# An attention and mixture-of-experts layer on one core: the hand-written order at the seam of two attention stages is changed, with a DMA's queue and a normalisation's place

## The chip, the cores and the metric

The kernel runs on 1 core of one Trainium2 chip. The metric is the device time of one execution, in microseconds (us): median 461.74 of 3 runs (461.70 to 462.92).

## The reference, cut to what matters

```python
# x (8,112,256), ctx (8,375,256), 16 heads; all float32
x = layernorm(x + self_attention(x, w_qkv, w_out, b_out))        # head width 64
x = layernorm(x + cross_attention(x, ctx, ctx, mask, Wq, bq, Wk, bk, Wv, bv, Wo, bo))  # head width 16
logits = x @ router.T; e = argmax(logits)                        # 8 experts, top 1
x = layernorm(x + down[e] @ (silu(gate[e] @ x) * (up[e] @ x)) + shared_expert(x))
```

## The kernel before, in words

Each engine has its own program; semaphores join them, and an engine runs its program strictly in order. The order in which the pieces stand in each program is therefore the schedule. T = 896 tokens are 8 batch elements of 112 rows, or NT = 7 tiles of 128 rows.

**Self-attention** is a loop over b = 0..7 on every engine. In one pass TensorE (PE) does `score1(0,b)`, then `out1(b-2)` (the output projection of tile b-2, 16 instructions, from b = 2 on), `between1(b,0)`, `score1(1,b)`, `between1(b,1)`, then four `turn`s (transposes of the probabilities of four heads each) with `between1(b,2..5)` between them, `value1(0,b)` ahead of `turn(2)` and `value1(1,b)` at the end. `between1` holds work for later stages: for b < 6 the next q, k, v of self-attention; at b = 6 the first k and v of cross-attention; at b = 7 `turn_x1` of the first tiles (the transposed, normalised result), the first query projection `project_q(0)` and one `project_k`. VectorE (DVE) does `rowmax`, `normalise` (a reciprocal and a multiplication), `evac_pt` (copies a turned tile out of PSUM) and the layernorm of tile b-2 in two halves: `ln1_a` (add, statistics, eps; then GpSimd takes the inverse root) and `ln1_b`. ScalarE (ACT) does the exponentials `exps(g,b)` and copies out of PSUM: `evac_o`, `evac_x1`, `evac_k`.

`query_scale` on DVE (L1122) makes the factor by which `evac_q` multiplies the queries. It reads the result of one small matmul (L564), which lies in the same PSUM bank as `out1`'s; `prep` 7 says it is done, and `out1(0)` waits for it.

**Cross-attention** is a loop over 32 slots n = 4b + g. In a slot PE does `score2(n)`, `turn2_(n-1,0)` and `(n-1,1)`, work of place 0, `turn2_(n-1,2)` and `(n-1,3)`, work of places 1 and 2, `value2(n-2)`. Place 1 waits for `max2` of the slot's third strip (L671), since `project_v` of place 1 writes that strip's bank. DVE does four `mask_and_max(n,r)` with `between(n,place)` among them and then `evac_pt2(n-1)`, for which the next `score2` waits. ACT does the exponentials `exps2(n,r)` and three of the four `evac_pt`. For b = 0 `between_first` holds the rest of the queries' preparation: tiles 3 to 6 of `turn_x1` and `project_q(1)`. They share one PSUM bank (`PE_M2`), so each waits for the copy of the one before.

For b >= 1, in slot g = 2, DVE copies the former element's output (`evac_ot`), PE turns it (`turn_o`), and DVE divides it by its sums (`normalise2`, L1215: a reciprocal and a multiplication).

After that come the router, the shared expert, and a loop over the routed tiles; the change does not touch them.

The inputs come by DMA. SyncE (SP) issues nearly all: first eight parts of `wqkv`. ACT issues one, the first two batch elements of `xT`. The first matmul needs that and the first part of `wqkv`.

Of the kernel before, what the change touches and what calls it, by code (L numbers as in the profile page):

```python
# [20 lines left out]
B, S, C = 8, 112, 256  # L21
# [30 lines left out]
def build(nc, a, out):  # L52
    ctx = ExitStack()
    with ctx:
# [193 lines left out]
        def _(sp):  # L248
            for u in range(8):
                sp.dma_start(wqkv[:, :, 256 * u:256 * u + 256], a["wqkv"][:, :, 256 * u:256 * u + 256]).then_inc(w_qk[u], 16)  # L250
# [136 lines left out]
        def _(pe):  # L387
# [78 lines left out]
            def out1(t):  # L466
                pe.wait_ge(ot1[1], t + 2)
                pe.wait_ge(ot1[0], t + 2)
                if t == 0:
                    pe.wait_ge(w_loaded["out"], 16)  # L470
                    pe.wait_ge(prep, 7)
                else:
                    pe.wait_ge(y1, t)
                for k in range(8):
# [10 lines left out]
            def project_q(i, M=PE_M2):  # L485
                pe.wait_ge(x1t_sb, 5 if i == 1 else min(-(-(i + 1) * S_PAIR // TILE), NT))
# [20 lines left out]
            def between1(b, c):  # L507
# [18 lines left out]
                elif c == 2:  # L526
                    pe.wait_ge(x1t_sb, 1)
                    project_v(2, 0, J)
                elif c == 3:
                    project_q(0, J)  # L530
                elif c == 4:
                    pe.wait_ge(v_sb, KT)
                    project_k(0, 1, J)
                else:
                    pe.wait_ge(q_sb, 1)
                    turn_x1(2, J)
# [5 lines left out]
            for b in range(B):  # L542
# [19 lines left out]
                if b == 1:  # L562
                    pe.wait_ge(prep, 5)
                    pe.matmul(PE_W1[:, 0:S], anyw, ident[0:S, 0:S], start=True, stop=True).then_inc(q_any, 1)  # L564
# [3 lines left out]
            def score2(n):  # L568
# [3 lines left out]
                if n == 0:  # L572
                    pe.wait_ge(exp1[2], B)
                    pe.wait_ge(exp1[3], B)
                    pe.wait_ge(k_sb, KC + 1)
                    pe.wait_ge(x1t_sb, 3)
# [12 lines left out]
            def turn2_(n, r):  # L589
                pe.wait_ge(exp2, n * STRIPS + r + 1)  # L590
                if n == 0 and r == 0:
                    pe.wait_ge(pt1, 4 * B)
                elif n == 0 and r == 1:
                    pe.wait_ge(y1, NT)
# [52 lines left out]
            def between_first(g, place):  # L647

                if (g, place) == (0, 0):
                    pe.wait_ge(ot1[1], B)  # L650
                    project_k(1, 1)
                if (g, place) == (1, 0):
                    pe.wait_ge(k_sb, 2 * KC)
                    turn_x1(3)
                if (g, place) == (1, 2):
                    pe.wait_ge(x1t_sb, 4)
                    turn_x1(4)
                if (g, place) == (2, 0):
                    project_q(1)
                if (g, place) == (2, 2):  # L660
                    pe.wait_ge(q_sb, 2)
                    turn_x1(5)
                if (g, place) == (3, 0):
# [231 lines left out]
        def _(act):  # L895
# [41 lines left out]
            act.dma_start(xT[:, :, 0:S_PAIR], a["xT"][:, :, 0:S_PAIR]).then_inc(xT_loaded[0], 16)  # L937
            for c in range(2):
                evac_v(c, 0)
            for b in range(B):  # L940
# [16 lines left out]
                if b == B - 1:  # L957
                    evac_k(0, 1, PE_J1[0])
                    evac_x1(2, PE_J1[1])
# [15 lines left out]
            def before_exps(n):  # L975

                b, g = n // GROUPS, n % GROUPS
                if b == 0 and g >= 2:
                    evac_x1(g + 2)
# [3 lines left out]
            def between(n, place):  # L983

                b, g = n // GROUPS, n % GROUPS
                if (g, place) == (0, 0) and b == 0:
                    evac_k(1, 1)
                if (g, place) == (1, 0) and b == 0:
                    evac_x1(3)
                if (g, place) == (3, 0) and b == 0:  # L990
                    evac_x1(6)
# [478 lines left out]
```

## Time and profile before

| | |
|---|---|
| time, 3 runs | 461.74, 462.92, 461.70 us |
| the profiled execution: its own time / its span | 461.74 / 460.0 us |
| PE busy | 416.0 us, 90% of the span |
| DVE, ACT, GpSimd busy | 242.0, 194.8, 37.8 us |
| self-attention, about | 5 to 170 us |
| cross-attention, about | 170 to 340 us |

The page divides the span in 40 slices. A digit is the busy share of the slice in tenths:

```profile
PE   5998999999999988999999999999899999999910
DVE  1366666656656637575666565757724622222225
ACT  1063353433534528676666656676741010111200
PEclk9999999999999999999999999999999999999975
```

PE is the engine to watch. Its work overlaps itself (a matmul begins before the one ahead has ended), so a stretch is without gaps when the rows of PE follow each other with no bracket. A bracket at the end of a row is the idle time ahead of it and what ended that.

### The profile page before, as it was taken

The numbers are of one execution on the slowest core, as the hardware profiler recorded it, in microseconds if no ns is written. First come the engines' busy times: TensorE is split into PE (matmuls) and PEld (weight loads), VectorE is DVE, ScalarE is ACT, GpSimd is POOL, SyncE is SP. The second block draws the span as 40 slices with busy tenths as digits, with TensorE's granted clock in tenths as the row PEclk, the third lists the DMA queues.
The fourth block names the chain that finished last, engine by engine and source line by source line (L and its number), as shares of the span: only waits on it lengthen the run. The fifth ranks groups of instructions, "written<-read, shape, count | busy, mean of one in ns | idle before, by whom it ended". The sixth has DMA issues, their size and how long they took to land.

```text
span 460.0 us, 8866 instructions
## 1 busy us (share of the span) xinstructions
PE 416.0 (90%) x3119; PEld 294.9 (64%) x3120; DVE 242.0 (53%) x709; ACT 194.8 (42%) x580; POOL 37.8 (8%) x59
## 2 busy tenths in 40 slices
PE   5998999999999988999999999999899999999910
PEld 5865878778786766676666666766654656555510
DVE  1366666656656637575666565757724622222225
ACT  1063353433534528676666656676741010111200
POOL 3010010110101001000010100101000320000043
PEclk9999999999999999999999999999999999999975
DMA  7993000000000102124040406500000120111123
GB/s 257 359 389 107 1 1 1 0 2 1 1 1 1 34 21 119 66 105 167 8 170 3 171 2 216 232 1 1 2 1 0 36 70 11 36 35 46 34 68 114
DMA packets 16137, 33.29 MB, mean 72 GB/s; under 512 B 2096, under 2 KB 10784, under 8 KB 14816
## 3 DMA queue, kind: packets, MB, share of 16 engines
q1 hardware_dynamic: 15152, 30.68, 18.4%
q0 software_dynamic: 672, 1.84, 1.3%
q8 instruction: 25, 0.41, 0.4%
q10 hardware_dynamic: 272, 0.23, 0.2%
q14 instruction: 16, 0.13, 0.1%
HBM read 26.97 MB, written 5.77 MB: 71 GB/s over the span
## 4 chain that ended last, share of the span: by engine, by line
PE 78%; DVE 9%; issue 4%; DMA 3%; POOL 3%; ACT 2%; DVEq 0%; POOLq 0%; SPq 0%; ACTq 0%
PE bank L603 11%; PE bank L405 9%; PE bank L419 6%; PE bank L585 6%; PE bank L475 6%; PE bank L503 5%; PE bank L497 4%; PE bank L825 4%; PE bank L849 3%; PE bank L831 3%; PE bank L462 3%; PE bank L619 3%; PE bank L759 3%; PE bank L436 3%; PE bank L448 2%
## 5 line engine op out<-in xcount | busy, mean ns | idle before, releaser
L1199 DVE CUSTOM_DVE_ANT_0 p<-bank,mask 112x375 f32<-112x375 f32 x128 | 62.8, 546 | 33.7 <-PE bank L585 33.7
L965 ACT ACTIVATE p<-p,nm 112x375 f32<-112x375 f32 x128 | 74.7, 608 | 6.7 <-DVE nm L1199 6.7
L603 PEld LDWEIGHTS bank<-ident,p 112*125 112x125 f32 x384 | 48.9, 187 | 22.5 <-issue 18.0
L972 ACT ACTIVATE pT<-bank 125x336 f32<-125x336 f32 x96 | 42.8, 447 | 47.5 <-PE bank L603 47.5
L603 PE MATMUL bank<-ident,p 112*125 112x112 f32 x384 | 59.6, 287 | 1.3
L405 PE MATMUL bank<-x2T,arena 128*128 128x224 f32 x256 | 54.7, 362 | 5.2 <-DMA arena<-in_wqkv 5.2
L908 ACT ACTIVATE p<-bank,nm 112x112 f32<-112x112 f32 x128 | 43.6, 366 | 18.6 <-DVE nm L1073 18.6
L405 PEld LDWEIGHTS bank<-x2T,arena 128*128 128x128 f32 x256 | 47.9, 196 | 5.2 <-DMA x2T<-in_xT 4.8
L1066 DVE TENSOR_SCALAR arena<-bank 128x448 f32<-128x448 f32 x32 | 20.0, 624 | 28.7 <-PE bank L405 28.6
L585 PE MATMUL bank<-kT,qz 32*112 32x375 f32 x256 | 28.8, 517 | 4.3 <-DVE pT L1207 2.4
L339 POOL TENSOR_TENSOR rstd<-veps,minus_half 128x1 f32<-128x1 f32 x14 | 7.7, 550 | 303.5 <-DVE veps L1099 303.5
L419 PE MATMUL bank<-arena,x2T 128*112 128x512 f32 x64 | 30.5, 604 | 0.0
L1073 DVE TENSOR_REDUCE nm<-bank 112x4 f32<-112x448 f32 x32 | 19.2, 620 | 20.0 <-PE bank L436 20.0
L914 ACT ACTIVATE arena<-bank 128x448 f32<-128x448 f32 x16 | 8.7, 544 | 48.7 <-PE bank L462 48.7
L908 ACT ACTIVATION_READ_ACCUMULATOR p<-bank,nm 112x1 f32 x128 | 28.1, 219 | 0.0
L475 PE MATMUL bank<-arena 128*128 128x256 f32 x112 | 26.0, 385 | 1.0 <-ACT arena L914 0.6
L503 PE MATMUL bank<-wx,mid 128*125 128x256 f32 x96 | 26.5, 399 | 0.0
L759 PE MATMUL bank<-x2T,ugs 128*128 128x512 f32 (+1 forms) x64 | 25.5, 543 | 0.6 <-DVE pT L1280 0.4
L619 PEld LDWEIGHTS bank<-pT,v 125*32 125x32 f32 x768 | 17.3, 109 | 12.1 <-issue 9.0
L619 PE MATMUL bank<-pT,v 125*32 125x112 f32 x768 | 25.0, 263 | 0.0
L1040 ACT ACTIVATE p<-bank 128x512 f32<-128x512 f32 x9 | 5.4, 597 | 45.5 <-PE bank L825 45.5
L497 PE MATMUL bank<-mid,wx 128*128 128x375 f32 x64 | 23.3, 485 | 1.3 <-DVE qz L1141 1.3
(135 smaller groups left out, 574.9 us busy)
## 6 DMA issues: line engine op xcount, KB each, us to landing
arena<-in_ug SPq DMA_DIRECT2D x8, 1024.0 KB, 6.1
arena<-in_dn SPq DMA_DIRECT2D x8, 512.0 KB, 7.0
mid<-in_ctxT SPq DMA_DIRECT2D x8, 375.0 KB, 3.3
arena<-in_wqkv SPq DMA_DIRECT2D x8, 256.0 KB, 5.1
slots_x<-zeros SPq DMA_DIRECT2D x14, 128.0 KB, 7.2
kT<-slots_x SPq DMA_DIRECT2D x9, 128.0 KB, 2.0
slots_y<-p SPq DMA_DIRECT2D x9, 128.0 KB, 1.7
arena<-in_wqkv SPq DMA_DIRECT2D x2, 512.0 KB, 6.3
```

Source lines behind the costliest of these rows:

```text
L405: mm = pe.matmul(J[:, m * S_PAIR:(m + 1) * S_PAIR], wqkv[:, k, col:col + 128], xT[:, k, i * S_PAIR:(i + 1) * S_PAIR], start=(k == 0), stop ...
L419: mm = pe.matmul(PE_J1[c][0:S, :], xT[:, k, b * S:(b + 1) * S], wqkv[:, k, 2 * INNER + 512 * c:2 * INNER + 512 * (c + 1)], start=(k == 0), ...
L475: mm = pe.matmul(PE_W1[:, 0:C], oT1[:, k, t * TILE:(t + 1) * TILE], wout[:, k, :], start=(k == 0), stop=(k == 7))
L497: mm = pe.matmul(M[:, 0:S2], wx[:, 1, k, m * 128:(m + 1) * 128], ctxT[:, b % 2, k, :], start=(k == 0), stop=(k == KC - 1))
L503: mm = pe.matmul(M[0:SK, 0:C], ctxT[:, b % 2, k, t * SK:(t + 1) * SK], wx[:, 2, k, :], start=(k == 0), stop=(k == KC - 1))
L585: mm = pe.matmul(PE_S2[r][0:S, 0:S2], qz[rows_r, b // 2 % 2, m, par, b % 2, :], kT2[rows_r, b % 2, m, :], start=True, stop=True)
L603: mm = pe.transpose(PE_T2[r][0:SK, t * S:(t + 1) * S], p2[i % RING][:, t * SK:(t + 1) * SK], ident[0:S, 0:S])
L619: mm = pe.matmul(PE_V2[VP * r:VP * r + VP, g * S:(g + 1) * S], v2[:, b % 2, t, g * STRIPS + r, :], pT2[0:SK, (n * STRIPS + r) % RING, t, : ...
L908: e = act.activation(p1[g][:, n, :], PE_S1[g % 2][0:S, n * S:(n + 1) * S], ACT.Exp, bias=nm1[:, h:h + 1], accum_out=rs1[:, h:h + 1])
L965: act.activation(p2[i % RING], p2[i % RING], ACT.Exp, bias=nm2[:, i % H:i % H + 1], scale=-1.0).then_inc(exp2, 1)
L972: act.activation(pT2[0:SK, i % RING], PE_T2[r][0:SK, 0:KT * S].rearrange("p (k n) -> p k n", k=KT), ACT.Copy).then_inc(pt2_act, 1)
L1199: v.tensor_tensor_reduce(p2[i % RING], PE_S2[r][0:S, 0:S2], bias[:], 1.0, 3e38, ALU.add, ALU.min, accum_out=nm2[:, i % H:i % H + 1]).then_ ...
```

## The change

Six things change.

1. The first `xT` load is issued by SP, ahead of the eight parts of `wqkv`, and no longer by ACT.
2. The small matmul for `query_scale` moves from the end of b = 1 to the end of b = 6, `query_scale` from the end of b = 1 to the head of b = 7. `out1(0)` does not wait for it any more; `out1(5)` does.
3. In the self-attention loop DVE does `ln1_a` ahead of `normalise(0)` and `ln1_b` ahead of `evac_pt(0)`. `ln1_a(6)` and `ln1_b(6)` come right behind the loop, ahead of the first `mask_and_max`; before, they stood in slots 0 and 1.
4. At b = 7 the places of `between1` become: `project_q(0)`, `project_v(2,0)`, `project_k(0,1)`, `project_k(1,1)`. The DVE and ACT programs follow: `evac_q(0)` now stands ahead of `normalise(2)` and `evac_pt(1)`, `evac_v(2,0)` ahead of `normalise(3)`.
5. `project_k(1,1)` leaves slot 0; `turn_x1(2)` enters it, and `turn_x1(3..6)` and `project_q(1)` come one to three places earlier. `evac_q(1)` moves from slot 2 to slot 1 on DVE, the `evac_x1` on ACT with their tiles. The first `score2` waits for both halves of k of elements 0 and 1.
6. `normalise2` moves from the end of slot g = 2 (behind `evac_pt2`) to the place between its second and third `mask_and_max`.

```diff
@@ block.sync
+            sp.dma_start(xT[:, :, 0:S_PAIR], a["xT"][:, :, 0:S_PAIR]).then_inc(xT_loaded[0], 16)
@@ out1(t), PE
                 if t == 0:
                     pe.wait_ge(w_loaded["out"], 16)
-                    pe.wait_ge(prep, 7)
                 else:
                     pe.wait_ge(y1, t)
+                if t == NT - 2:
+                    pe.wait_ge(prep, 7)
@@ project_q
-                pe.wait_ge(x1t_sb, 5 if i == 1 else min(-(-(i + 1) * S_PAIR // TILE), NT))
+                pe.wait_ge(x1t_sb, min(-(-(i + 1) * S_PAIR // TILE), NT))
@@ between1(b = 7, c), PE
                 elif c == 2:
-                    pe.wait_ge(x1t_sb, 1)
+                    project_q(0, J)
+                elif c == 3:
+                    pe.wait_ge(x1t_sb, 2)
                     project_v(2, 0, J)
-                elif c == 3:
-                    project_q(0, J)
                 elif c == 4:
-                    pe.wait_ge(v_sb, KT)
+                    pe.wait_ge(q_sb, 1)
                     project_k(0, 1, J)
                 else:
-                    pe.wait_ge(q_sb, 1)
-                    turn_x1(2, J)
+                    pe.wait_ge(v_sb, 3)
+                    project_k(1, 1, J)
@@ PE, end of pass b
-                if b == 1:
+                if b == B - 2:
                     pe.wait_ge(prep, 5)
+                    pe.wait_ge(y1, b - 1)
                     pe.matmul(PE_W1[:, 0:S], anyw, ident[0:S, 0:S], start=True, stop=True).then_inc(q_any, 1)
@@ score2(0)
-                    pe.wait_ge(k_sb, KC + 1)
-                    pe.wait_ge(x1t_sb, 3)
+                    pe.wait_ge(v_sb, KT)
+                    pe.wait_ge(k_sb, 2 * KC)
@@ turn2_
-                if n == 0 and r == 0:
+                if n == 0 and r < 2:
+                    pe.wait_ge(y1, NT)
                     pe.wait_ge(pt1, 4 * B)
-                elif n == 0 and r == 1:
-                    pe.wait_ge(y1, NT)
@@ between_first(g, place), PE
                 if (g, place) == (0, 0):
                     pe.wait_ge(ot1[1], B)
-                    project_k(1, 1)
+                    turn_x1(2)
+                if (g, place) == (0, 2):
+                    pe.wait_ge(x1t_sb, 3)
+                    turn_x1(3)
                 if (g, place) == (1, 0):
-                    pe.wait_ge(k_sb, 2 * KC)
-                    turn_x1(3)
+                    project_q(1)
                 if (g, place) == (1, 2):
-                    pe.wait_ge(x1t_sb, 4)
+                    pe.wait_ge(q_sb, 2)
                     turn_x1(4)
                 if (g, place) == (2, 0):
-                    project_q(1)
+                    pe.wait_ge(x1t_sb, 5)
+                    turn_x1(5)
                 if (g, place) == (2, 2):
-                    pe.wait_ge(q_sb, 2)
-                    turn_x1(5)
-                if (g, place) == (3, 0):
                     pe.wait_ge(x1t_sb, 6)
                     turn_x1(6)
@@ ACT
-            act.dma_start(xT[:, :, 0:S_PAIR], a["xT"][:, :, 0:S_PAIR]).then_inc(xT_loaded[0], 16)
...
                 if b == B - 1:
-                    evac_k(0, 1, PE_J1[0])
-                    evac_x1(2, PE_J1[1])
+                    for m in range(KC):
+                        evac_k(m, 1, PE_J1[m])
...
-                if b == 0 and g >= 2:
-                    evac_x1(g + 2)
+                if b == 0 and g >= 1:
+                    evac_x1((3, 4, 6)[g - 1])
...
                 if (g, place) == (0, 0) and b == 0:
-                    evac_k(1, 1)
-                if (g, place) == (1, 0) and b == 0:
-                    evac_x1(3)
-                if (g, place) == (3, 0) and b == 0:
-                    evac_x1(6)
+                    evac_x1(2)
+                if (g, place) == (2, 0) and b == 0:
+                    evac_x1(5)
@@ DVE, pass b
             for b in range(B):
+                if b == B - 1:
+                    query_scale()
                 rowmax(0, b)
                 rowmax(1, b)
-                normalise(0, b)
                 if b >= 2:
                     ln1_a(b - 2)
+                normalise(0, b)
                 rowmax(2, b)
                 normalise(1, b)
                 rowmax(3, b)
-                evac_pt(0, b)
                 if b >= 2:
                     ln1_b(b - 2)
+                evac_pt(0, b)
...
                 if b == B - 1:
-                    evac_v(2, 0, PE_J1[0])
+                    evac_q(0, PE_J1[0])
                 normalise(2, b)
                 evac_pt(1, b)
...
                 if b == B - 1:
-                    evac_q(0, PE_J1[1])
+                    evac_v(2, 0, PE_J1[1])
                 normalise(3, b)
...
-                if b == 1:
-                    query_scale()
+            ln1_a(NT - 1)
+            ln1_b(NT - 1)
@@ DVE, between(n, place)
-                if n == 0 and place == 3:
-                    ln1_a(NT - 1)
-                if n == 1 and place == 1:
-                    ln1_b(NT - 1)
...
-                if (g, place) == (1, 2) and b in (2, 4):
+                if (g, place) == (1, 2) and b in (0, 2, 4):
                     evac_q(b // 2 + 1)
-                if (g, place) == (2, 2) and b == 0:
-                    evac_q(1)
...
-                if (g, place) == (2, 4) and b >= 1:
+                if (g, place) == (2, 1) and b >= 1:
                     normalise2(b - 1)
```

## Rows read from the trace of the kernel before

**Rows 1.** Busy time by stretch, inside self-attention: stretch, length, busy of each engine, clock, DMA

```profile
90.00:120.00 30.00, 29.92 (x219) 24.01 (x216) 17.51 (x38) 11.64 (x54) 1.26 (x2) 1.00 0.01 2
```

**Rows 2.** The start, timeline: start, duration, engine, line; last row, DMA queues of 2 to 3 us

```profile
0.80 5.51 SPq L250 DMA_DIRECT2D arena<-in_wqkv  x8
...
5.22 7.05 PE L405 MATMUL bank<-x2T,arena 128*128 128x224 f32 x27 [5.22 <-DMA arena<-in_wqkv]
...
q10 hardware_dynamic: 115, 0.10, 48.8%
```

**Rows 3.** The small matmul and the out1 behind it, timeline; last row from the chain of waits

```profile
56.41 0.47 PE L564 MATMUL bank<-ident,oT 112*128 112x112 f32 x2
...
58.20 3.69 PE L475 MATMUL bank<-arena 128*128 128x256 f32 x16 [0.34 <-DVE qscale L1129]
...
76.26 0.97 PE bank L436 x16
```

**Rows 4.** The last pass of self-attention, b = 7, timeline; one row from the chain of waits

```profile
155.06 0.42 DVE L1092 TENSOR_TENSOR ybuf<-bank,xb 128x256 f32<-128x256 f32 x1 [0.68 <-PE bank L475]
156.39 0.62 DVE L1073 TENSOR_REDUCE nm<-bank 112x4 f32<-112x448 f32 x1
158.38 0.40 ACT L924 ACTIVATE x1T<-bank 128x256 f32<-128x256 f32 x1
159.38 1.69 PE L489 MATMUL bank<-x1T,wx 128*128 128x224 f32 x8
161.00 0.99 PE L462 MATMUL bank<-pT,arena 112*64 112x112 f32 x16
161.11 1.28 DVE L1141 SCALAR_TENSOR_TENSOR qz<-bank,cols,qscale 128x448 f32<-128x448 f32 x2 [0.35 <-PE bank L489]
163.05 0.62 DVE L1087 COPY pT<-bank 112x448 f32<-112x448 f32 x1
...
162.51 1.28 PE bank L497 x4
...
165.10 0.99 PE L462 MATMUL bank<-pT,arena 112*64 112x112 f32 x16 [0.50 <-DVE pT L1087]
166.73 3.72 PE L475 MATMUL bank<-arena 128*128 128x256 f32 x16 [0.64 <-ACT arena L914]
```

**Rows 5.** Slots 0 to 4 and one later layernorm, timeline

```profile
171.51 0.55 DVE L1199 CUSTOM_DVE_ANT_0 p<-bank,mask 112x375 f32<-112x375 f32 x1 [6.46 <-PE bank L585]
173.62 0.90 PE L585 MATMUL bank<-kT,qz 32*112 32x375 f32 x8 [0.88 <-DVE nm L1199]
177.72 0.90 PE L585 MATMUL bank<-kT,qz 32*112 32x375 f32 x8
183.62 0.90 PE L585 MATMUL bank<-kT,qz 32*112 32x375 f32 x8
188.41 0.90 PE L585 MATMUL bank<-kT,qz 32*112 32x375 f32 x8 [0.27 <-DVE pT L1207]
...
336.50 0.41 DVE L1229 TENSOR_SCALAR xres<-ybuf,mv,rstd 128x256 f32<-128x256 f32 x1 [0.66 <-POOL rstd L339]
```

**Rows 6.** Slot 14 (b = 3, g = 2), timeline

```profile
266.32 0.60 PE L626 MATMUL bank<-ident,oT 128*112 128x128 f32 x4
266.84 0.55 DVE L1199 CUSTOM_DVE_ANT_0 p<-bank,mask 112x375 f32<-112x375 f32 x1
267.45 1.12 PE L503 MATMUL bank<-wx,mid 128*125 128x256 f32 x4
269.37 0.25 DVE L1218 RECIPROCAL rc<-bank 112x16 f32<-112x16 f32 x1
269.55 0.90 PE L585 MATMUL bank<-kT,qz 32*112 32x375 f32 x8 [0.27 <-DVE pT L1207]
269.65 0.42 DVE L1220 TENSOR_TENSOR o<-bank,rc 112x256 f32<-112x256 f32 x1
```

**Rows 7.** Busy time by stretch, behind PE's last matmul

```profile
440.00:445.00 5.00, 0.00 (x0) 0.00 (x0) 0.00 (x0) 0.00 (x0) 1.98 (x3) 0.72 0.17 52
```

More of the change, by code:

```diff
@@ L1267, in _ @@
                     evac_pt2(n - 1)
-                between(n, 4)
             ln2_a(NT - 2)
```

## The prediction

> **What bounds the kernel now.** I read the page's engine shares, the busy time by stretch, the waits of PE, and then the timeline wherever the diff moves something. Inside self-attention PE has no gap: 29.92 of 30 us [rows 1]. There an edit on DVE or ACT is worth something only if it makes PE wait. At the seam PE does wait: for `evac_pt`, for `evac_o`, for the first `mask_and_max` (0.50, 0.64, 0.88 us in brackets) [rows 4, 5]. In the cross-attention slots PE looks full, but two links of DVE set its pace: `project_v` of place 1 begins at 267.45, just behind the end of the slot's third mask (266.84 + 0.55 = 267.39), and `score2` waits 0.27 for `evac_pt2` [rows 6]. The reader is to see in these rows that a DVE delay ahead of the third mask goes to PE one for one.
>
> All times below are on the clock of the profiled execution. Its span is 460.0 and its own time 461.74, which is also the median, so a change of the span is added to 461.74.
>
> **The start.** The move costs the SP queue one issue more; eight take 5.51, so 0.69 each. But between 2 and 3 us only the ACT queue's transfer moves data [rows 2]: the first part of `wqkv`, issued at 0.80 as well, waits behind `xT` already. Issued 0.69 later it is still there in time. I take 0; the bounds are -0.1 and +0.69. The later parts keep a lead: PE works the first 27 matmuls in 7.05 us without another wait. The Trainium skill (DMA: Bandwidth & Descriptors, section "Issuing engines are not separate DMA queues") says that a second issuing engine saves only issue time, because all transfers run on the same 16 engines. By that rule alone the move costs its issue time, and the sum would be 0.7 higher.
>
> **The small matmul and `query_scale`.** At b = 1 it takes from 56.41 to `out1(0)` at 58.20, 1.79; without it only `score1` lies ahead, 0.97 [rows 3]. So 0.82 is gained at b = 2. At b = 7 the same sequence stands ahead of `out1(5)`: the matmul, `query_scale` on DVE, PE waiting for `prep` 7. That is 0.82 again, and nothing hides it, since `out1(5)` is followed by `score1(1,7)` in PE's order. Net 0; bounds -0.82 (hidden at b = 7) and +0.4.
>
> **Layernorm ahead of `normalise(0)`, b = 2 to 6.** `ln1_a` still waits for `out1`. `normalise(0)` now follows it, and takes 0.75 (below) of the time in which DVE had nothing to do until the next scores; `turn(0)` comes two microseconds later, behind a `project_v1`. PE stays full [rows 1]: 0; bounds -0.1 and +0.5 in all.
>
> **The last pass, b = 7.** Here the cover is thin, since `project_v1` is replaced by short transposes. With the two 0.82 cancelled, the old times hold up to `out1(5)`.
> - `ln1_a(5)` runs 155.06 to 156.39 [rows 4]. `normalise(0)` used to be done by then; now it follows. Its length: from `evac_q` at 161.11 to `evac_pt(2)` at 163.05 are 1.94, evac_q is 1.28 less 0.09 overlap, so 0.75 for a normalise. `turn(0)` and `rowmax(2)` come 0.75 to 0.9 later, hence `exps(2)`, hence `evac_x1(1)`: 158.38 becomes 159.13, ends 159.5.
> - `project_q(0)`, now at place 2, needs that copy: it begins at 159.6 and ends at 161.27 (1.69). The old one began at 159.38, but behind `turn(1)` and `project_v`; these 0.34 and 0.9 now follow it on PE.
> - DVE now has `evac_q(0)` ahead of `normalise(2)` and `evac_pt(1)`. It begins at 161.3, `evac_pt(1)` 1.94 later at 163.25, and is done at 163.87. `value1(0)` needs it: 164.0 against 161.00, **+3.0**. This is the step I rest most on: a wait on a projection is put ahead of a copy for which PE is ready.
> - From `value1(0)` to `value1(1)` were 4.10, with a 0.50 wait, a short one ahead of `turn(3)` and `turn_x1(2)` (0.34). These go; `project_k(1,1)`, 1.28, comes: about 4.25. So `value1(1)` begins at 168.25 instead of 165.10, `out1(6)` at 169.88 instead of 166.73.
> I take **+3.15**; bounds +1.0 (the 1.28 alone, if DVE is hidden) and +4.
>
> **Slots 0 to 3.** `out1(6)` ends its 3.72 at 173.6. DVE now does the whole layernorm first: `ln1_a` 1.4, the root on GpSimd 0.66 of idle, `ln1_b` 0.45 [rows 4, 5]. The first mask is at 176.16 instead of 171.51: +4.65, of which 1.50 new. Behind DVE stand all masks, behind them ACT and PE. Before, those two halves lay where DVE waited for scores anyway. `turn_x1(3)`, at place 2 of slot 0, waits for `evac_x1(2)`, which ACT does behind two exponentials: `score2(1)` comes 0.28 later still, at 178.55 (old: 173.62). Slot 1 then has `project_q(1)` and `evac_q(1)` and grows from 4.10 to some 5.55: mask 3 is behind `evac_q`, `evac_pt2` behind it. Slot 2 loses them, 5.90 to 4.88. Together +0.43; if slot 1 takes the whole 5.90, +0.78. Slot 3 loses a transpose and gains nothing, for its `project_v` waits for the third mask. Sum **+2.2**; bounds +0.7 and +3.
>
> **`normalise2`, seven times.** At place 1 it stands behind the second mask. It must wait for `turn_o`, 266.32 + 0.60 = 266.92, where the third mask began at 266.84. Reciprocal to multiplication is 0.28, the multiplication 0.42 less overlap 0.08: the third mask begins at 266.95 + 0.28 + 0.34 = 267.57, 0.73 later [rows 6]. `project_v` goes from 267.45 to 268.18, its copy, `evac_pt2` and the next `score2` with it. Where `normalise2` stood, behind `evac_pt2`, DVE had idle time ahead of the next scores, so nothing comes back. At b = 7 there is no `project_v`, but `evac_pt2` is pushed in the same way. 7 x 0.73 = **+5.1**; bounds 0 (if PE's own work ends as late as the mask) and +6.3 (0.9 each, with hand-overs).
>
> **The sum**: 0 + 0 + 0 + 3.15 + 2.2 + 5.1 = +10.5: 461.74 + 10.5 = **472.2 us**.
>
> **Rivals.**
> - *`normalise2` is hidden.* For it: PE's row at 267.45 has no idle bracket, so PE might have been busy to that very moment and have slack behind. Against it: `score2` has a bracket that names DVE. Time: 472.2 - 5.1 = 467.1. Chance 11%.
> - *The seam is hidden, `normalise2` is not.* If ACT and DVE at b = 7 have more slack than I read, only the moved work remains (+1): 461.74 + 5.1 + 1 = 467.8. Chance 9%.
> - *TensorE's clock falls at the seam.* PE has nothing from the end of `turn_x1(2)`, about 174.7, to `turn_x1(3)` at 178.2. Behind PE's last matmul (439.1) the granted clock is 1.00 to past 440 and 0.72 on the mean of 440 to 445, so it went from 2.4 to 1.2 GHz near 442.2, 3 us after the last work [rows 7]. The gap is as long as that. Then slots 1 and 2 start at half rate; a slot's 4.8 us has 1.5 to 2 us that hang on matmuls in the chain, so +1.7: 473.9. Against it: the clock never falls inside the old trace. Chance 13%. The Trainium skill (TensorE: Matmul & The Clock Gate, section "HAM oscillation — how this bites in real kernels") has the same rule, that gaps in PE's work make the next work run cold; whether this gap is enough, no row of the old trace shows.
> - *The other side: faster.* The two gaps behind `evac_pt` and `evac_o` at b = 7 (0.50 and 0.64) and the 0.88 at `score2(1)` are 2.0. If `project_k(1,1)`, 1.28, drops into them, and the 0.82 at b = 7 is hidden, and `normalise2` costs nothing, the time is 461.74 - 2.1 = 459.6. It decides at one place: whether `evac_pt(1)` is ready when PE comes to `value1(0)`. For it: the idle is really there. Against it: `evac_q` waits for PE and then holds DVE 1.2 us ahead of that copy. Chance 4%.
>
> **How the numbers follow.** The forecast has 57%, with its own range 469.5 to 474; the rivals 11, 9, 13 and 4%; no change that can be measured 2%; slower by some other amount 4%. The range 467 to 474.5 takes in the two partial cases and the clock, and leaves out mainly the fast side. Within 0.3% (1.4 us, about what a measurement of this kernel can tell from no change): 3%. Faster: 4%. Slower: 93%.
>
> **What would show it.** In the new trace: `out1(0)` follows `score1(0,2)` without a bracket, `out1(5)` has one that names `qscale`; the copy into pT1 ahead of `value1(0,7)` begins about 2 us behind `evac_q(0)` and PE waits for it 1 us or more; the first mask is 2.5 us behind the end of `out1(6)`; slot 1 is longer than slot 2; in every slot 4b + 2 the third mask comes 0.7 later behind the second than the others do, and slots g = 2 last 5.5 instead of 4.8. The prediction is wrong if slots g = 2 keep 4.8 us, or if PE at b = 7 has less than 1 us more idle than before.

## The result

| | before | after |
|---|---|---|
| median (range) of 4 runs, us | 462.33 (461.70 to 464.38) | 477.27 (476.61 to 477.88) |
| ratio, 95% interval | | 1.0315 (1.0277 to 1.0352) |
| the profiled execution: own time / span | 461.74 / 460.0 | 477.75 / 476.0 |
| its granted clock of PE, mean | 0.981 | 0.968 |

The change makes the kernel 3.2% slower. The forecast was 472.2 with a range up to 474.5: the sign is right, the size is not, and 477.27 lies outside the range. Where the clock does not fall, the forecast's steps come to 11.1 us instead of its 10.5; what it lacked is a drop of TensorE's clock, twice.

### The profile page after: what moved, and what is told of

Same layout as the page of the kernel before. It is cut to its first block, busy times and chain, and to the rows that moved or that the text cites. A ratio compares the mean times of both kernels' runs of the same rounds, so it can differ in the third digit from the quotient of the medians.

```text
span 476.0 us, 8866 instructions
## 1 busy us (share of the span) xinstructions
PE 423.3 (89%) x3119; PEld 299.2 (63%) x3120; DVE 242.7 (51%) x709; ACT 194.8 (41%) x580; POOL 38.0 (8%) x59
## 4 chain that ended last, share of the span: by engine, by line
PE 74%; issue 9%; DVE 9%; POOL 3%; DMA 3%; ACT 2%; DVEq 0%; SPq 0%; POOLq 0%; ACTq 0%
PE bank L605 10%; PE bank L406 9%; PE bank L588 6%; PE bank L420 6%; PE bank L505 5%; PE bank L477 5%; PE bank L499 4%; PE bank L827 3%; PE bank L851 3%; PE bank L833 3%; PE bank L621 3%; PE bank L761 3%; PE bank L437 3%; PE bank L463 3%; PE bank L449 2%
## 5 line engine op out<-in xcount | busy, mean ns | idle before, releaser
L505 PE MATMUL bank<-wx,mid 128*125 128x256 f32 x96 | 27.6, 411 | 3.5 <-DVE nm L1200 3.5
L621 PEld LDWEIGHTS bank<-pT,v 125*32 125x32 f32 x768 | 17.3, 109 | 12.8 <-issue 10.5
```

What stands on the lines that cost most here:

```text
L505: mm = pe.matmul(M[0:SK, 0:C], ctxT[:, b % 2, k, t * SK:(t + 1) * SK], wx[:, 2, k, :], start=(k == 0), stop=(k == KC - 1))
L621: mm = pe.matmul(PE_V2[VP * r:VP * r + VP, g * S:(g + 1) * S], v2[:, b % 2, t, g * STRIPS + r, :], pT2[0:SK, (n * STRIPS + r) % RING, t, : ...
```

## The profile after

The page, three of its lines (span; busy time and instructions by engine; the granted clock in 40 slices of 11.9 us):

```profile
span 476.0 us, 8866 instructions
PE 423.3 (89%) x3119; PEld 299.2 (63%) x3120; DVE 242.7 (51%) x709; ACT 194.8 (41%) x580; POOL 38.0 (8%) x59
PEclk9999999999999797999999999999999999999985
```

The clock's row was a flat 9 before, up to its last two slices. Now it has a 7 in the 14th slice (155 to 167 us) and another in the 16th (178.5 to 190): exactly the two stretches that the diff rearranges. PE is busy 7.3 us more, though it has no more to compute: at half clock the same matmuls last longer.

**The start.** Timeline, first matmul (start, length, engine, line, operation; the bracket is the idle time ahead and what ended it):

```profile
5.41 1.08 PE L406 MATMUL bank<-x2T,arena 128*128 128x224 f32 x2 [5.41 <-DMA arena<-in_wqkv]
```

Before it was at 5.22, but in the sixteen profiled executions it lies between 4.76 and 5.50: 4.76 to 5.41 in the ten with the load on SP, 5.08 to 5.50 in the six with it on ACT. No cost can be read here.

**The last pass, b = 7.** Timeline, to hold against [rows 4]. There `out1(5)` starts at 151.30 and here at 151.58, so count from it.

```profile
151.58 3.69 PE L477 MATMUL bank<-arena 128*128 128x256 f32 x16 [0.34 <-DVE qscale L1128]
157.51 0.60 PE L449 MATMUL bank<-ident,p 112*112 112x112 f32 x4 [0.68 <-DVE p L1080]
159.35 0.40 ACT L926 ACTIVATE x1T<-bank 128x256 f32<-128x256 f32 x1
159.80 3.36 PE L491 MATMUL bank<-x1T,wx 128*128 128x224 f32 x8 [1.70 <-ACT x1T L926]
163.20 1.28 DVE L1140 SCALAR_TENSOR_TENSOR qz<-bank,cols,qscale 128x448 f32<-128x448 f32 x2 [3.07 <-PE bank L491]
165.13 0.62 DVE L1086 COPY pT<-bank 112x448 f32<-112x448 f32 x1
165.81 1.05 PE L463 MATMUL bank<-pT,arena 112*64 112x112 f32 x16 [0.17 <-DVE pT L1086]
171.89 3.72 PE L477 MATMUL bank<-arena 128*128 128x256 f32 x16 [0.64 <-ACT arena L916]
```

`project_q(0)` starts where the forecast put it (159.80; forecast 159.6, plus 0.28 of offset). Then it takes 3.36 instead of 1.69. All that follows hangs on it: DVE waits 3.07 for its result, then `evac_q`, then the copy for `value1(0)`. The busy time by stretch says why (columns: stretch, length, busy time of PE, PEld, DVE, ACT, POOL, granted clock, DMA share, GB/s):

```profile
154.90:161.00 6.10, 3.72 (x29) 2.84 (x28) 4.54 (x12) 3.36 (x18) 0.55 (x1) 0.85 0.00 1
160.00:165.00 5.00, 5.00 (x15) 4.31 (x16) 1.89 (x5) 1.09 (x7) 0.00 (x0) 0.50 0.00 0
181.00:186.00 5.00, 5.00 (x21) 3.66 (x21) 1.49 (x6) 2.45 (x6) 0.00 (x0) 0.50 0.02 7
186.00:187.00 1.00, 1.00 (x7) 0.96 (x6) 0.04 (x1) 0.00 (x0) 0.00 (x0) 0.77 0.00 0
```

0.50 is the lower level, 1.2 GHz. In the first of these stretches PE is busy 3.72 of 6.10 us; in the same stretch of before it was busy 4.97. But 1.20 of the 3.72 are `project_q(0)`, already at the lower clock: ahead of the fall, from 154.90 to 159.30, PE is busy 2.52 of 4.40 us, where before it was busy 3.27.

By stretches of a tenth of a microsecond the clock falls at 159.15, 1.05 us into the wait of 1.70, and at 179.63, 2.8 us into the wait of 3.70. So it falls while PE waits, before the slow matmuls begin. It comes back at 165.98 and 186.46: the lower level lasts 6.8 us both times.

**Slots 0 to 2**, timeline, to hold against [rows 5]:

```profile
175.54 0.90 PE L588 MATMUL bank<-kT,qz 32*112 32x375 f32 x8
177.71 0.82 DVE L1106 TENSOR_SCALAR xres<-ybuf,mv,rstd 128x256 f32<-128x256 f32 x1 [0.66 <-POOL rstd L340]
178.45 0.54 DVE L1200 CUSTOM_DVE_ANT_0 p<-bank,mask 112x375 f32<-112x375 f32 x1
180.50 0.66 PE L484 MATMUL bank<-ident,xres 128*128 128x128 f32 x2 [3.70 <-DVE nm L1200]
181.09 1.61 PE L588 MATMUL bank<-kT,qz 32*112 32x375 f32 x8
184.02 2.90 PE L491 MATMUL bank<-x1T,wx 128*128 128x224 f32 x8
189.22 0.90 PE L588 MATMUL bank<-kT,qz 32*112 32x375 f32 x8 [0.47 <-DVE pT L1208]
194.01 0.90 PE L588 MATMUL bank<-kT,qz 32*112 32x375 f32 x8
```

The first mask is 2.84 behind the end of `out1(6)` (forecast 2.5). PE waits 3.70 (forecast 3.5), the clock falls, and `score2(1)`, eight matmuls that take 0.90 elsewhere, takes 1.61; `project_q(1)` takes 2.90 where the same eight matmuls took 1.69 before (at 179.30). Slots 0 to 3 last 5.55, 8.13, 4.79 and 4.80; before 3.24, 4.10, 5.90 and 4.79.

**Slot 6 (g = 2)**, timeline, to hold against [rows 6]; the first row is its `score2`, the last that of slot 7:

```profile
209.40 0.90 PE L588 MATMUL bank<-kT,qz 32*112 32x375 f32 x8
211.61 0.26 DVE L1219 RECIPROCAL rc<-bank 112x16 f32<-112x16 f32 x1
211.90 0.42 DVE L1221 TENSOR_TENSOR o<-bank,rc 112x256 f32<-112x256 f32 x1
212.25 0.54 DVE L1200 CUSTOM_DVE_ANT_0 p<-bank,mask 112x375 f32<-112x375 f32 x1
212.85 1.13 PE L505 MATMUL bank<-wx,mid 128*125 128x256 f32 x4 [0.58 <-DVE nm L1200]
214.95 0.90 PE L588 MATMUL bank<-kT,qz 32*112 32x375 f32 x8 [0.27 <-DVE pT L1208]
```

Reciprocal and multiplication lie ahead of the third mask, and `project_v` waits 0.58 for that mask where [rows 6] has no bracket. The slot lasts 5.55 instead of 4.80. Six slots do so, and slot 30, at b = 7, goes from 3.62 to 4.38.

## The experiments

Each kernel below is the kernel after or the kernel before with one thing changed, or several where that is said. A filler is a 128x128 matmul of the identity with itself into a free PSUM bank (two MATMUL instructions in the profile); nothing reads its result, it only occupies PE while it would wait.

### A. Does the clock cost what the trace suggests?

The theory: each fall is due to PE's idle time ahead, and without the falls the kernel after comes to the forecast's 472. The rival: the falls are an effect of something else, or the matmuls' length hides behind DVE, and the fillers bring nothing.

`a_fill_both`, on the kernel after:

```diff
@@ between1(b = 7, c), PE
                 elif c == 2:
+                    pe.wait_ge(x1t_sb, 1)
+                    filler(8, J)
                     project_q(0, J)
@@ between_first(0, 0), PE
                     turn_x1(2)
+                    pe.wait_ge(pt1, 4 * B)
+                    filler(18, bank[4])
```

> The changed kernel with matmuls that compute nothing of use in PE's two long gaps: 8 of 128 columns ahead of project_q(0) at b = 7 and 18 behind turn_x1(2) in slot 0; the order and every wait stay. Theory 'clock': the granted clock stays 1.00 through the seam, project_q(0) takes 1.5 us and slot 1 about 5.6 instead of 8.1, and the time falls by 4 to 5.5 us to 472 to 473.5. Rival 'waits alone': the excess over the forecast is in waits that were read wrongly; then the time stays within 1.5 us of 477.3 or grows.

Measured: 472.93 (472.66 to 473.57, 4 runs), 4.3 us less than after. Timeline and busy time by stretch (PE alone) of it:

```profile
158.18 1.96 PE L391 MATMUL bank<-ident 128*128 128x128 f32 x16
160.04 1.78 PE L495 MATMUL bank<-x1T,wx 128*128 128x224 f32 x8
170.49 3.72 PE L481 MATMUL bank<-arena 128*128 128x256 f32 x16 [0.64 <-ACT arena L924]
175.24 4.18 PE L391 MATMUL bank<-ident 128*128 128x128 f32 x36
179.57 0.90 PE L594 MATMUL bank<-kT,qz 32*112 32x375 f32 x8
181.15 1.69 PE L495 MATMUL bank<-x1T,wx 128*128 128x224 f32 x8
185.13 0.90 PE L594 MATMUL bank<-kT,qz 32*112 32x375 f32 x8 [0.47 <-DVE pT L1216]
```
```profile
154.90:161.00 6.10, 5.42 (x48) 1.00 0.00 1
160.00:165.00 5.00, 3.61 (x29) 1.00 0.18 58
180.00:186.00 6.00, 4.76 (x39) 1.00 0.00 1
```

With PE occupied the clock stays at 1.00, `project_q` is back at 1.7 to 1.8, `score2(1)` at 0.90. `out1(6)` begins 18.68 behind `out1(5)` (forecast 18.58; after 20.31), and from there to `score2(4)` are 24.23 (forecast 23.9; after 26.92). So the two falls cost 1.63 and 2.69, 4.32 together, as much as the difference of the medians, and the forecast's steps hold within 0.4 us each once they are gone. PE's wait ahead of `value1(0)` is 1.39 here, as the forecast had it.

`a_fill_slot0`: only the second of the two edits.

```diff
                     turn_x1(2)
+                    pe.wait_ge(pt1, 4 * B)
+                    filler(18, bank[4])
```

> The changed kernel with only the 18 idle-time matmuls in slot 0. Theory 'clock': the fall at b = 7 stays (project_q(0) near 3.2 us), the fall in slot 0 goes, slot 1 lasts about 5.6 us; the time falls by about 3 us to 474.3. Rival 'waits alone': no fall of more than 1 us.

Measured: 473.82 (472.08 to 474.94). The four runs are 472.1 and 472.7 with a mean clock of 0.983, and 474.9 twice with 0.979. The profiled one had no fall at b = 7 either, so that fall doesn't come in every execution of this kernel, and the expected `project_q(0)` near 3.2 was not seen. Slot 1 is 5.56. The row of `project_q(0)`:

```profile
159.16 1.78 PE L495 MATMUL bank<-x1T,wx 128*128 128x224 f32 x8 [1.70 <-ACT x1T L932]
```

This row says more than the fillers do. The wait is the same 1.70 as in the kernel after, no filler stands in it, and the clock stays up: `out1(6)` is 18.67 behind `out1(5)`, as with the fillers (18.68). So the fillers themselves cost nothing, and 1.63 is the price of the fall. But the wait alone does not bring the fall: with the same wait the clock falls in one execution and not in another. That the 8 fillers prevent it is likely and not shown by traces: all runs of `a_fill_both` are at 472.7 to 473.6, against two of four here at 474.9.

### B. The price of each reordering

`a_n2back`: the kernel after, `normalise2` back behind `evac_pt2`.

```diff
-                if (g, place) == (2, 1) and b >= 1:
+                if (g, place) == (2, 4) and b >= 1:
                     normalise2(b - 1)
...
                     evac_pt2(n - 1)
+                between(n, 4)
```

> The changed kernel with normalise2 back behind evac_pt2 (part 6 of the change undone). Theory 'gate': the third mask of seven slots comes 0.75 earlier and PE with it, slots g = 2 last 4.80 us again, the time falls by 7 x 0.75 = 5.3 to about 472.0. Rival 'shifted elsewhere': the slots are bound by something else as well, and less than 3 us comes back (474.5 or more).

Measured: 471.37 (469.11 to 472.37, 6 runs), 5.9 less than after; the slots g = 2 are 4.80 again. The profiled execution (469.14) has no fall at b = 7, behind a wait of 1.69 (`out1(6)` 18.66 behind `out1(5)`). It has the one at slot 0, but for 3.4 us only; there it costs 1.49 (from `out1(6)` to `score2(4)` 25.72, with no fall 24.23). What the slower runs have at b = 7 no trace shows.

`b_n2move`: the kernel before with only this move.

```diff
-                if (g, place) == (2, 4) and b >= 1:
+                if (g, place) == (2, 1) and b >= 1:
                     normalise2(b - 1)
```

> The kernel before with part 6 alone: normalise2 between the second and the third mask. Theory 'gate': 5.2 us slower than the kernel before, some 467.4; slots g = 2 last 5.55 us. Rival: the cost shows only together with the other parts, and this is within 1.5 us of the kernel before.

Measured: 468.51 (467.14 to 469.73, 4 runs), ratio 1.0138 (1.0107 to 1.0169). The slots are 5.55. Two runs are at 467.1 and 467.4 and two at 469.6 and 469.7, with the mean clock 0.982 and 0.978. The profile is of an execution in which the clock fell (busy time by stretch, PE alone),

```profile
41.50:43.80 2.30, 1.06 (x3) 1.00 0.01 4
44.00:49.00 5.00, 4.38 (x20) 0.66 0.01 3
```

at b = 1, a place that no diff touches, behind a wait of 2.05 that the kernel before has as well. The wait, in the kernel before:

```profile
43.75 1.04 PE L436 MATMUL bank<-arena 64*112 64x112 f32 x16 [2.05 <-ACT p L908]
```

From these scores to `out1(0)` are 14.45 in the kernel before and 16.07 here: this fall, of 3.4 us, costs 1.62. The faster pair against before's seven runs at 0.980 or 0.981 (median 461.83) is 467.27 - 461.83 = 5.4; the forecast had 5.1.

`f_ln6back`: the kernel after with the 8 fillers at b = 7, and `ln1_a(6)`, `ln1_b(6)` back in slots 0 and 1.

```diff
-            ln1_a(NT - 1)
-            ln1_b(NT - 1)
@@ between(n, place), DVE
+                if n == 0 and place == 3:
+                    ln1_a(NT - 1)
+                if n == 1 and place == 1:
+                    ln1_b(NT - 1)
```

> The changed kernel with the 8 idle-time matmuls at b = 7, and ln1_a(6) and ln1_b(6) back in slots 0 and 1 of VectorE's order. Theory 'layernorm on the way': the first mask comes 1.15 us behind the start of score2(0) instead of 2.9, PE's gap in slot 0 is half as long, so the clock stays up without idle-time matmuls there; against the kernel with both fillings (472.93) some 1.3 us less, 471.6. Rival 'the projection order': slot 1 absorbs it, and the time stays within 0.5 us of 472.9.

Measured: 472.05 (471.11 to 475.89), and in the trace slots 0 and 1 at 3.53 and 5.69 instead of 5.43 and 5.56: 1.77 less, with no fall and without the 18 fillers. So the layernorm ahead of the first mask is what opens the gap in which the clock fell. One of the four runs is at 475.89 with a mean clock of 0.976; where its clock fell no trace shows.

The next three stand against `a_fill_both` (fillers at both places):

`f_evq_behind`: `evac_q(0)` behind `normalise(2)` and `evac_pt(1)`.

```diff
-                if b == B - 1:
-                    evac_q(0, PE_J1[0])
                 normalise(2, b)
                 evac_pt(1, b)
+                if b == B - 1:
+                    evac_q(0, PE_J1[0])
```

> The changed kernel with both fillings, and evac_q(0) behind normalise(2) and evac_pt(1) in VectorE's order. Theory 'projection ahead of a copy': PE's wait ahead of value1(0,7) goes, value1(0,7) begins 1.3 us earlier, 471.6. Rival: project_k(0,1), which waits for q_sb, takes the wait over and the time stays at 472.9.

Measured: 472.00 (471.90 to 472.71). `value1(0)` comes 11.19 behind `out1(5)` instead of 12.66, and `out1(6)` 17.40 instead of 18.68:

```profile
162.94 0.99 PE L467 MATMUL bank<-pT,arena 112*64 112x112 f32 x16
169.15 3.72 PE L481 MATMUL bank<-arena 128*128 128x256 f32 x16 [0.64 <-ACT arena L924]
```

`f_norm0_first`: at b = 7 alone `normalise(0)` ahead of `ln1_a(5)`.

```diff
+                if b == B - 1:
+                    normalise(0, b)
                 if b >= 2:
                     ln1_a(b - 2)
-                normalise(0, b)
+                if not (b == B - 1):
+                    normalise(0, b)
```

> The changed kernel with both fillings, and normalise(0) ahead of ln1_a at b = 7 alone. Theory: turn(0), rowmax(2), exps(2) and evac_x1(1) come 0.75 earlier, project_q(0) with them: 472.1. Rival: the idle-time matmuls or turn(0) hide it, 472.9.

Measured: 473.42 (471.51, 471.70, 475.13, 475.83; mean clock 0.981 in the first two, 0.977 in the others). The trace says what the times can't: `value1(0)` 11.92, `out1(6)` 17.94 behind `out1(5)`, 0.74 less, one normalise.

`f_query_back`: the small matmul, `query_scale` and the wait for `prep` 7 back at b = 1.

```diff
@@ out1(t), PE
                 if t == 0:
                     pe.wait_ge(w_loaded["out"], 16)
+                    pe.wait_ge(prep, 7)
...
-                if t == NT - 2:
-                    pe.wait_ge(prep, 7)
@@ PE, end of pass b
-                if b == B - 2:
+                if b == 1:
                     pe.wait_ge(prep, 5)
-                    pe.wait_ge(y1, b - 1)
...
@@ DVE: query_scale from the head of b = 7 to the end of b = 1
```

> The changed kernel with both fillings, and the small matmul and query_scale back at b = 1, out1(0) waiting for prep 7. The forecast's 'net 0': out1(0) 0.8 later, out1(5) 0.8 earlier than in the kernel with fillings; 472.9 within 0.3. Rival 'hidden on one side': 0.8 more or less.

Measured: 472.62 (472.39 to 473.91), against 472.93 with them at b = 6 and 7: within the runs' spread. In the trace `out1(0)` to `out1(5)` is 93.10 again, against 93.95 with them at b = 6 and 7. So the 0.8 is paid at one place or the other.

`a_dve_back`: no fillers, all four DVE reorderings of the kernel after undone together (`normalise2`, `ln1(6)`, `evac_q(0)`, `normalise(0)` at b = 7); PE's new order stays.

```diff
@@ DVE: the edits of a_n2back, f_ln6back, f_evq_behind and f_norm0_first
```

> The changed kernel with VectorE's four reorderings undone (normalise2, the last layernorm, evac_q(0) behind evac_pt(1), normalise(0) ahead of ln1_a at b = 7), no fillings; TensorE's and ScalarE's new order, the start and query_scale stay. Theory 'VectorE's order and the clock behind it are nearly all of it': 463.5 to 465. Rival 'the projections' new places cost as much': 467 or more.

Measured: 467.27 (465.27 to 468.64, 6 runs), ratio 1.0097 (1.0066 to 1.0129). That is 10.0 less than after: two thirds of the loss come from DVE's order, with the falls that went with it. The time is above the 463.5 to 465 that I expected and just inside the rival, 467 or more, so what is left of the change isn't free. Part of it is the clock (mean 0.970 to 0.977 in the six runs); PE in the profile, by stretch:

```profile
159.00:162.50 3.50, 3.35 (x10) 0.55 0.00 0
```

In that execution (466.11; its span is 4.4 us above that of before) from `out1(5)` to `out1(6)` are 18.34, 2.91 more than before, of which `project_q(0)` at the lower clock makes 1.40 (3.18 instead of 1.78). From there to `score2(4)` are 22.46, 0.78 more than before, with no fall. So PE's new order has a price of its own of some 2 us, an estimate: 2.91 - 1.40 + 0.78 = 2.3, less what else the fall lengthened.

`b_start`: the kernel before with the `xT` load issued by SP.

```diff
+            sp.dma_start(xT[:, :, 0:S_PAIR], a["xT"][:, :, 0:S_PAIR]).then_inc(xT_loaded[0], 16)
-            act.dma_start(xT[:, :, 0:S_PAIR], a["xT"][:, :, 0:S_PAIR]).then_inc(xT_loaded[0], 16)
```

> The kernel before with part 1 alone: the first xT load on SP. The forecast's step: 0 to 0.7; with the changed kernel's trace (first matmul at 5.41 instead of 5.22) 0.2 us: 462.1 against 461.9. Rival: by the issue time alone, 0.7.

Measured: 463.31 in the median of 12, but six are at 461.35 to 462.58 (clock 0.981) and six at 464.0 to 464.4 (0.977), as before's own runs also split (22 of the 29 beside it at 461.5 to 462.7, seven at 464.4 to 465.0). Ratio 1.0009 (0.9988 to 1.0031): no cost that can be told, though the interval alone would still hold 0.7. Against it speak the runs at the higher clock (median 462.15 against 462.27) and the starts of the first matmul given above, none of which is 0.7 later with the load on SP.

### C. A version that beats both

`b_query_hidden`: the kernel before; at b = 1 the small matmul stands ahead of `score1(1,1)`, where PE waits anyway, and `query_scale` ahead of `rowmax(2,1)`.

```diff
+                if b == 1:
+                    pe.wait_ge(prep, 5)
+                    pe.matmul(PE_W1[:, 0:S], anyw, ident[0:S, 0:S], start=True, stop=True).then_inc(q_any, 1)
                 score1(1, b)
...
-                if b == 1:
-                    pe.wait_ge(prep, 5)
-                    pe.matmul(PE_W1[:, 0:S], anyw, ident[0:S, 0:S], start=True, stop=True).then_inc(q_any, 1)
@@ DVE
+                if b == 1:
+                    query_scale()
                 rowmax(2, b)
...
-                if b == 1:
-                    query_scale()
```

> The kernel before with the small matmul ahead of score1(1,1), where TensorE waits 2 us, and query_scale ahead of rowmax(2,1), where VectorE waits 1.7. Theory: the 0.82 at b = 2 goes, 461.1 against 461.9, and runs in which the clock falls at b = 1 may be rarer. Rival: the score matmuls then wait for query_scale's column, no gain.

Measured: 461.28 (460.52 to 464.25, 12 runs), 0.9972 (0.9951 to 0.9993). Eleven of the twelve are at a mean clock of 0.981 to 0.983, one, the 464.25, at 0.977. Without those at the lower clock the medians are 461.25 against 462.27 for the kernel before: 1.0 less, about the 0.8 forecast.

`b_best`: this, and `evac_pt2` ahead of the copy of `project_v`, since [rows 6] show `score2` waiting 0.27 for it:

```diff
-                between(n, 3)
                 if n >= 1:
                     evac_pt2(n - 1)
+                between(n, 3)
```

> As the one with query_scale in the idle time, and evac_pt2(n-1) ahead of evac_v at place 3 in VectorE's order. Theory: score2 waits 0.27 us for evac_pt2 in some 14 slots, behind a copy that itself waits for project_v; turned round, 3.5 us go: 457.6. Rival: score2 then waits for the copy (v_sb) as long, 461.1.

Measured: 460.44 (458.61 to 462.08, 12 runs), 0.9946 (0.9924 to 0.9969). That is far from the 457.6 expected, for two reasons. Six slots g = 2 and slot 28 last 4.54 instead of 4.80, slots 3 and 7 last 4.48, but the other slots g = 3 keep their 5.32 and slot 2 grows by 0.15: 2.3 in all, where I had counted on 14 slots and 3.5. And half of the runs fall: six are at 458.6 to 459.5 (clock 0.980 or 0.981), six at 461.3 to 462.1 (0.976, one 0.979). The faster six have the median 458.95, against 461.25 for the eleven of `b_query_hidden`: 2.3 again. Slot 6, timeline (the last row is the `score2` of slot 7):

```profile
203.80 0.50 DVE L1207 COPY pT<-bank 125x336 f32<-125x336 f32 x1
204.64 0.42 DVE L1148 TENSOR_TENSOR v<-bank,rows 125x256 f32<-125x256 f32 x1 [0.33 <-PE bank L503]
205.32 0.90 PE L585 MATMUL bank<-kT,qz 32*112 32x375 f32 x8
```

DVE waits 0.33 for `project_v` now, but PE has no bracket.

`b_fill_b1`: the kernel before with 8 fillers in the wait at b = 1, to see whether that wait is what splits its runs.

```diff
                     between1(b, 1)
+                if b == 1:
+                    filler(8, PE_W1)
                 score1(1, b)
```

> The kernel before with 8 matmuls of 128 columns that compute nothing of use in TensorE's 2 us wait ahead of score1(1,1). Theory 'the wait at b = 1 makes the second group': no run has a mean clock under 0.98 and none is over 463; the median stays at 461.9 or falls to it. Rival 'the fall comes from elsewhere' (the start, or the chip as a whole): a fourth of the runs or more stay at 464.3 to 465.0.

Busy time of that stretch (all engines), of before and then of `b_fill_b1`:

```profile
41.50:43.80 2.30, 0.25 (x3) 0.08 (x2) 0.80 (x2) 2.30 (x15) 0.00 (x0) 1.00 0.02 4
```
```profile
41.50:43.80 2.30, 2.03 (x19) 1.81 (x17) 0.80 (x2) 2.30 (x15) 0.00 (x0) 1.00 0.01 4
```

Measured: 462.54 (461.67 to 463.99, 12 runs), 1.0006 (0.9987 to 1.0024). No run has a mean clock under 0.979 any more, and none is above 464, while 4 of before's 22 were at 464.5 to 465.1 with 0.976 or 0.977. So the fall is gone, but five of the twelve stand at 463.4 to 464.0 with a clock of 0.980 or 0.981, where the theory had none over 463. The median is no better, and why is open; the profiled execution is one of the other seven. A candidate is in the traces: PE's first 64 matmuls, from 5 us on, last between 13.72 and 15.27 us, in a stretch that none of these diffs touches.

`b_best_fill`: `b_best` with the same fillers.

```diff
                 if b == 1:
+                    filler(8, PE_W1)
                     pe.wait_ge(prep, 5)
```

> The better version (query_scale in the idle time of b = 1, evac_pt2 ahead of evac_v) with the same 8 matmuls ahead of the small one. Theory 'the wait at b = 1': its slower group (461.3 to 462.1) is gone and all runs are at 458.6 to 459.6. Rival 'from elsewhere': half of the runs stay above 461.

Measured: 459.78 (459.65 to 461.29, 11 runs), 0.9951 (0.9934 to 0.9969): the lowest median here, 0.5% below before. The theory had all runs at 458.6 to 459.6; none is that low, and three are above 460.5. No mean clock is under 0.980. Against `b_best` alone the gain is steadiness and not speed: the intervals of the two ratios overlap, and the six faster runs of `b_best` lie below all of these.

## Why the prediction missed

By its own steps, with what was measured. "Order" is the part that is left when the clock doesn't fall (from `a_fill_both`).

| step | forecast | measured |
|---|---|---|
| start | 0 | none to be told (`b_start`) |
| small matmul, `query_scale` | 0 (-0.82 + 0.82) | 0 (`f_query_back`); from `out1(0)` to `out1(5)` +0.87 |
| layernorm order, b = 2 to 6 | 0 | 0: that stretch is 93.97 against 93.10, all of it the 0.87 ahead of `out1(5)` |
| b = 7, order | +3.15 | +3.25 |
| b = 7, clock | none (no rival either) | **+1.63** |
| slots 0 to 3, order | +2.2 | +2.55 |
| slots 0 to 3, clock | none (rival: +1.7) | **+2.69** |
| `normalise2`, seven times | +5.1 | +5.26 |
| sum | +10.5 | +15.4; the spans differ by 16.0 |

`normalise2`: 6 x 0.75 + 0.76 = 5.26. The sum: 3.25 + 1.63 + 2.55 + 2.69 + 5.26 = 15.38. Of the 0.6 left to 16.0, 0.28 lie ahead of `out1(5)`; the rest is unassigned. All this is the profiled execution, with a mean clock of 0.968; the four timed ones are at 0.972 to 0.974, so their falls may have been other ones, at nearly the same time (476.61 to 477.88).

**What failed is the term for TensorE's clock.** The sum has none for it; it stands only as a rival, "TensorE's clock falls at the seam", at 13% and +1.7. The falls cost 1.63 and 2.69, 4.32 us in the profiled execution. The rest of the sum is 0.6 too low.
- *The place.* I looked for one gap, the one in slot 0, as long as the 3 us behind PE's last matmul [rows 7]. I had worked out a second opening myself: in the step on b = 7 `project_q(0)` comes behind nothing but short transposes and a copy of ACT. The trace after has PE busy 2.52 of the 4.40 us there. I priced its waits and not what they do to the clock.
- *The rule.* My only row of a fall was behind a full stop of PE, and I looked for such a stop. The fall at b = 7 came behind a wait of 0.68, 0.60 of transposes and 1.05 us of the next wait. The one in slot 0 came 2.8 us into its wait, as behind the last matmul. The Trainium skill (TensorE: Matmul & The Clock Gate, section "HAM oscillation — how this bites in real kernels") has the direction right, gaps in PE's work make what follows run cold, and the trace agrees: 2.90 instead of 1.69 behind the gap of 3.70. By that, the rival deserved a higher chance for slot 0. The same page's section "A second HAM failure mode: psum-queue depth-cycling" tells of short idles between groups of matmuls that also cost the clock. That is nearer to b = 7, where the granted clock is 0.50 with no wait over 1.70, and I hadn't weighed it. Whether it is the same effect no run here shows.
- *The price.* I counted 1.5 to 2 us of matmuls in one slot's chain. The lower level lasted 6.8 us both times (and 3.4 in each of the four other traces that have a fall before the router), and what ran in it was on the path: `project_q(0)` 1.67 longer, `project_q(1)` 1.21, `score2(1)` 0.71. At half clock the matmuls on the path take up to twice as long; that alone would have given 1.7 for b = 7.

**What was right.** `project_q` put ahead of a copy that PE is ready for (`evac_q(0)` ahead of `evac_pt(1)`) is the largest part at b = 7 that was taken apart: 1.28 of 3.25 by `f_evq_behind`, and 0.74 is the normalise, by `f_norm0_first`. The other 1.23 no run separates. Without a fall `value1(0)` is 12.66 behind `out1(5)` instead of 9.70, so +2.96; the forecast had +3.0. `normalise2` ahead of the third mask goes to PE one for one, 0.75 for 0.73. Of the signs named ahead, `out1(5)`'s bracket that names `qscale`, the third mask 0.7 later and the slots of 5.5 are there. Two came otherwise: slot 1 is longer than slot 2, but by 3.34 and not 0.7, for the clock's sake; and PE's wait ahead of `value1(0)` is 0.17 and not 1, since the time went into a slow `project_q` and not into a wait; it is 1.39 in the traces with no fall. For the same reason one of the two signs that were to prove the forecast wrong came: from `out1(5)` to `out1(6)` PE is idle 3.20 against 2.29 before, less than 1 us more. With no fall (`a_fill_slot0`) it is 4.41, 2.1 more. That is how a fall looks in a timeline: the brackets are small and the same rows are up to twice as long.

**A smaller miss.** Slots 0 to 3 are 0.35 above forecast. `ln1_b(6)` took 0.82 in the chain ahead of the first mask, against 0.45 in the sum.

## What to carry to other kernels

When a reordering opens waits on TensorE, add the waits' effect on its clock to the range and the chances, as a term that some executions have and others not: take the stretch ahead, see how little work is left in it, and count the matmuls on the path behind it up to twice. Here one fall cost between 1.5 and 2.7 us. A vector instruction put ahead of a link for which TensorE is ready costs its full length each time, even if the engine is only half busy; and the wait that remains in brackets tells which link that is, as `evac_pt2` here, whose place ahead of another copy gained 2.3 us in executions with no fall (0.8 in the medians). Where a kernel's times split in two groups, look at the granted clock of each run before reading a difference of 2 us.

## What the hardware showed that I had not expected

- The clock fell in a partly idle stretch, with 1.05 us of a wait gone and PE busy 2.52 of 4.40 us. It then stayed at 0.50 for 6.8 us, though PE had no wait but one of 0.17 from 159.80 on, and came back in the midst of work.
- Whether it falls can differ between executions of one kernel. A wait of 2.05 us at b = 1 is in the kernel before; 18 of its 22 runs in the last comparison show no sign of a fall, and 4 are 2.5 to 3.1 us above the median of the others, with a mean clock of 0.976 or 0.977 and not 0.981. The fall at b = 1 alone is 1.62 of that (`b_n2move`); the two traces that have it are also 1.0 us longer than that of before, or more, in the first 64 matmuls (15.05 and 15.27 against 14.05).
- 26 fillers took 4.3 us off a kernel (`a_fill_both`) without any of its own work changed.
- `ln1_b`'s one instruction (128x256) takes 0.40 to 0.41 us for tiles 0 to 5 in both kernels. It took 0.53 for tile 6 in the kernel before, 0.82 in the kernel after and 0.99 in `f_ln6back`, the three places where GpSimd makes two additions of 128x256 (1.43 to 1.48) at the same time. DMA traffic alone isn't the cause: it was 451 GB/s in the second case and 21 in the third, the longest. That GpSimd's additions are, is argued from these rows; no run took them away. The Trainium skill (GPSIMD Engine Reference, section "Specifications") says that GpSimd shares its SBUF interfaces with VectorE and gets in the way of some of VectorE's instructions; these rows agree as far as they go.

The stretch of that instruction in the kernel after, then its row and its stretch in `f_ln6back` (columns as above):

```profile
177.70:178.50 0.80, 0.00 (x0) 0.00 (x0) 0.79 (x2) 0.00 (x0) 0.80 (x2) 1.00 1.06 451
```
```profile
178.00 1.43 POOL L358 TENSOR_TENSOR xb<-xres,rows 128x256 f32<-128x256 f32 x2
...
178.59 0.99 DVE L1112 TENSOR_SCALAR xres<-ybuf,mv,rstd 128x256 f32<-128x256 f32 x1
```
```profile
178.60:179.60 1.00, 1.00 (x7) 1.00 (x6) 1.00 (x4) 1.00 (x3) 0.83 (x2) 1.00 0.07 21
```
